# Layer 0 of a two-layer kernel: the top two experts marked in place of indexed, value products in halves

## Chip, cores and metric

The kernel runs on one core of one Trainium2 chip. The metric is device time in microseconds of one launch. The engines are TensorE (PE; its weight loads are PEld), VectorE (DVE), ScalarE (ACT), GpSimd (POOL) and SyncE (SP), which issues most transfers.

## The reference, cut

Two post-norm layers over x of 16 x 512 tokens with 128 features. The change touches layer 0 alone: an attention over the 16 heads of each token (not over tokens), and a mixture of 8 experts of which the two with the largest logits count.

```python
# attention of layer 0, per token: 16 heads of 8
q, k, v = (qkv[..., :dh], qkv[..., dh:2 * dh], qkv[..., 2 * dh:])
scores = jnp.einsum('bnhd,bngd->bnhg', q, k) / SCALE
attn = jax.nn.softmax(scores, axis=-1)
out = jnp.einsum('bnhg,bngd->bnhd', attn, v)
# experts of layer 0
logits = jnp.einsum('bsd,ed->bse', x, gate_w) + gate_b
topv, topi = jax.lax.top_k(logits, K)                       # K = 2 of E = 8
keep = jax.nn.one_hot(topi, E, dtype=jnp.float32).sum(axis=-2)
logits = jnp.where(keep > 0, logits, -jnp.inf)
gate_score = jax.nn.softmax(logits, axis=-1)
out = jnp.einsum('bseo,bse->bso', expert_out, gate_score)
```

## The kernel before

`layer0` takes the 8192 tokens as 32 pairs of tiles of 128 tokens. Each engine has its own program, written out by hand as a function `step(u, j, part)`, and 32 steps (plus the filling and the emptying) run through `steps`; the middle ones are a hardware loop of two steps a turn. The stages are skewed: in the step in which pair s gets its scores, pair s-1 gets its value products and head sums, pair s-2 its gate and experts, pair s-3 its second norm. Within one engine the order is that of the calls in its `step`; between engines semaphores decide. A name ending in `_ready`, `_ps` or `_sb` is such a semaphore.

One step on DVE (L627 and below): the moments of the first norm (L640, L644, which wait for PE's `r1_ps`), sums of the exps and their reciprocal (L736, L743, for POOL), two products of queries and keys (L662, 4.4 us together), the moments of the second norm (L652, L656), the gate (L677 to L705), the sums of the products (L714), their maximum (L720) and the shift (L727).

The gate turns the 8 logits of each token of the two tiles (`ps_logits`, a part of the PSUM tile `ps_front`) into 8 gates. It finds the 8 largest of each tile in order (`dve.max`, L677), then their indices (`max_index`, L680, which is a load of the values and a search), casts the indices to f32 (L683), compares them with an iota (L689), makes the two softmax weights out of ACT's exp of the difference of the two largest (`gexp`, L533; L685, L694, L696), multiplies (L698) and adds over the two ranks (L705). The cast indices, the denominator and the weights are kept in PSUM. PE and ACT wait for `gates_ready`: ACT scales the expert products with the gates (`apply_gates`, L542), PE makes the second tile's expert products (`four_experts`, L396) when the first four gated tiles have left PSUM.

POOL makes the attention weights (`normalise`, L266) and then, per tile, one product of weights and values of 128 x 2048 (`pv_products`, L274), and between them the small steps of the norms (L288 to L310) and the residual's bias (L316). PE adds each tile's product over the heads with 16 transposing matmuls (`sum_heads`, L364), the first of which waits for the whole product; the sum goes through ACT (`copy_oT`, L505) to the projection (`project`, L377, L379), whose result DVE's next moments read.

## Time and profile before

| | us |
|---|---|
| median of 3 runs | 2190.77 (2188.96 to 2191.76) |
| profiled execution | 2186.65 |
| its span, first to last instruction | 2184.9 |
| layer 0 in the span | about 0 to 540 |
| PE, DVE, ACT, POOL busy over the whole span | 93%, 81%, 72%, 49% |

Each engine's busy share says how full it is, not whether it sets the end. For that one reads the timeline of each engine in one step and looks for the engine that never waits for another. A record's start and duration are in us; a number in square brackets is the idle time just before it and whose work ended it. Records of one engine may overlap by some hundredths of a us, since its instructions are pipelined. A merged row (x2) covers several instructions in sequence.

### The profile page before, as it was taken

Reading aid. Unit: us, or ns where it says so; the run is one execution under the profiler, and the core shown is the slowest. Engines: PE = TensorE matmul, PEld = TensorE weight load, DVE = VectorE, ACT = ScalarE, POOL = GpSimd, SP = SyncE. Lnnn points to the kernel's source line nnn. Section 1 sums busy time; section 2 is a strip of 40 time slices with the busy share of each in tenths; the row PEclk is TensorE's granted clock in tenths of the full one; section 3 lists DMA queues with packets and bytes.
Section 4 is the critical chain, followed back from the end, with each engine's and each line's share of the span. In section 5 each row is a group of like instructions: output and inputs, shape, how many; then the busy total and the mean of one; then the engine's idle time right before and its main releaser. Section 6 shows DMA issues by size and latency. Waiting matters only on the chain. (4 is left out here: it accounts for less than half of the span.)

```text
span 2184.9 us, 59761 instructions
## 1 busy us (share of the span) xinstructions
PE 2037.5 (93%) x16112; PEld 1524.8 (70%) x16112; DVE 1778.6 (81%) x5918; ACT 1563.4 (72%) x3951; POOL 1060.6 (49%) x2184
## 2 busy tenths in 40 slices
PE   7999999997999999999999999999999993999990
PEld 5666666664776776676676677677677663999990
DVE  7999999992888888888888888888888884777765
ACT  3666566665888877887887887887878782777774
POOL 6777878783124344334334334434434435444445
PEclk9999999998999999999999999999999996999995
DMA  2000000000000000000000000000200001222227
GB/s 77 23 29 22 29 22 29 24 24 23 2 2 12 2 12 12 4 9 11 7 7 12 9 4 12 12 2 11 89 2 12 12 3 42 64 65 64 67 59 231
DMA packets 63632, 62.84 MB, mean 29 GB/s; under 512 B 9834, under 2 KB 58613, under 8 KB 62855
## 3 DMA queue, kind: packets, MB, share of 16 engines
q1 hardware_dynamic: 54906, 42.64, 6.5%
q0 software_dynamic: 8448, 16.93, 2.2%
q8 instruction: 121, 1.98, 0.4%
q14 instruction: 157, 1.29, 0.2%
HBM read 33.17 MB, written 22.69 MB: 26 GB/s over the span
## 5 line engine op out<-in xcount | busy, mean ns | idle before, releaser
L1368 DVE SCALAR_TENSOR_TENSOR restT<-ps_t,leadT 128x512 f16<-128x512 f32 (+1 forms) x768 | 458.9, 597 | 136.5 <-ACT leadT L1295 106.4
L1295 ACT ACTIVATE leadT<-ps_t 128x512 f16<-128x512 f32 (+1 forms) x768 | 402.2, 524 | 134.4 <-PE ps_t L1169 133.4
L1152 PE MATMUL ps_s<-xT_all,qm 128*128 128x512 f32 (+1 forms) x1024 | 489.9, 560 | 0.8 <-ACT qm L1276 0.8
L1169 PEld LDWEIGHTS ps_t<-ident,p 128*128 128x128 f32 x2560 | 315.4, 141 | 234.0 <-issue 169.4
L1169 PE MATMUL ps_t<-ident,p 128*128 128x128 f32 x2560 | 413.5, 276 | 8.1 <-DVE restT L1368 6.1
L1286 ACT ACTIVATE p<-ps_s,neg_max 128x512 f32<-128x512 f32 (+1 forms) x512 | 325.6, 636 | 80.8 <-DVE neg_max L1358 67.7
L988 POOL CAST v_parts<-v_all 128x36 bf16<-128x36 f32 x256 | 57.3, 224 | 610.2 <-PE ps_o L1183 609.9
L1358 DVE CUSTOM_DVE_ANT_0 ps_s<-ps_s,mask 128x512 f32<-128x512 f32 (+1 forms) x512 | 319.8, 625 | 39.4 <-PE ps_s L1152 38.2
L1152 PEld LDWEIGHTS ps_low<-xT_all,qm 128*128 128x128 f32 x1024 | 194.8, 190 | 135.7 <-issue 122.4
L1143 PE MATMUL ps_qm<-xT_all,m_all 128*128 128x512 f32 x512 | 264.0, 597 | 2.7 <-PEq L766 2.7
L274 POOL TENSOR_TENSOR pv_prod<-probs,kv 128x2048 f32<-128x2048 f32 x64 | 259.5, 4076 | 3.8 <-POOL probs L266 2.3
L1669 POOL DMA_INDIRECT results<-row_out,row_in x136 | 133.6, 983 | 159.3 <-DVE row_out L1800 150.0
L1152 PE MATMUL ps_low<-xT_all,qm 128*128 128x256 f32 (+1 forms) x1024 | 209.0, 327 | 0.0
L1276 ACT ACTIVATE qm<-ps_qm,mb_all 128x512 f32<-128x512 f32 x256 | 176.0, 687 | 44.8 <-PE ps_qm L1143 41.4
L1286 ACT ACTIVATE p<-ps_low,neg_max 128x256 f32<-128x256 f32 (+1 forms) x512 | 187.9, 427 | 0.1
L1358 DVE CUSTOM_DVE_ANT_0 ps_low<-ps_low,mask 128x256 f32<-128x256 f32 (+1 forms) x512 | 177.2, 386 | 12.6 <-PE ps_low L1152 1.8
L1790 DVE SCALAR_TENSOR_TENSOR e_hid<-e_ps_u,e_wide,e_silu 114x128 f32<-114x128 f32 x408 | 118.3, 345 | 57.8 <-ACT e_silu L1749 57.2
L542 ACT ACTIVATE gated<-ps_y,gates 128x128 f32<-128x128 f32 x512 | 141.4, 372 | 31.0 <-DVE gates L705 29.3
L1183 PE MATMUL ps_o<-v_parts,leadT 128*128 128x27 bf16 x2560 | 161.5, 175 | 0.9 <-DVE restT L1368 0.5
L1183 PE MATMUL ps_o<-v_parts,restT 128*128 128x27 bf16 x2560 | 160.6, 174 | 0.0
L1074 POOL DMA_INDIRECT rows_dram<-rows,slot_idx x128 | 128.8, 1007 | 63.8 <-issue 50.3
L1749 ACT ACTIVATE e_silu<-e_ps_g,e_wide 114x128 f32<-114x128 f32 x408 | 120.0, 365 | 52.0 <-PE e_ps_g L1702 52.0
(231 smaller groups left out, 4144.2 us busy)
## 6 DMA issues: line engine op xcount, KB each, us to landing
row_in<-rows_dram SPq DMA_DIRECT2D x136, 65.0 KB
y<-results SPq DMA_DIRECT2D x16, 512.0 KB, 5.2
xT<-in_xT SPq DMA_DIRECT2D x32, 128.0 KB, 2.1
xres<-in_xT SPq DMA_DIRECT2D x32, 128.0 KB, 2.1
xT_all<-x2T SPq DMA_DIRECT2D x32, 128.0 KB, 2.0
out_x<-x SPq DMA_DIRECT2D x16, 256.0 KB, 3.4
xT_all<-in_wide SPq DMA_DIRECT2D x1, 2760.0 KB
results<-row_out,row_in POOLq DMA_INDIRECT x136
```

What stands on the lines that cost most here:

```text
L274: pool.tensor_tensor(tile(pv_prod, a, HH * DH).rearrange("p (g h d) -> p g h d", g=H, d=DH), tile(probs, a, HH).rearrange("p (h g) -> p g ...
L542: last = act.activation(tile(gated[a], e), tile(ps_y[half], e % 4), ACT.Copy, scale=gates[:, a * E + e:a * E + e + 1])
L1143: pe.matmul(ps_qm[:, :], blk(m_all, h), xT_all[:, bass.ds(b * S, S)], start=True, stop=True).then_inc(qm_ps, 1)
L1152: mm = pe.matmul(ps_s[n], qm[j][:, n * P:(n + 1) * P], xT_all[:, bass.ds(b * S, (n + 1) * P)], start=True, stop=True)
L1169: mm = pe.transpose(ps_t[g][:, at + n * P:at + (n + 1) * P], probs[i][:, n * P:(n + 1) * P], ident[:, :])
L1183: mm = pe.matmul(out_ps[:, i, :], part[:, at + n * P:at + (n + 1) * P], v_parts[j][:, n * PARTS * PV:(n + 1) * PARTS * PV], start=(n == 0 ...
L1276: act.activation(qm[j][:, :], ps_qm[:, :], ACT.Identity, bias=mb_all[:, h:h + 1], scale=SCALE).then_inc(qm_sb, 1)
L1286: act.activation(probs[i][:, :], ps_s[i], ACT.Exp, bias=neg_max[:, i:i + 1], scale=-1.0).then_inc(probs_ready[i], 1)
L1295: act.activation(leadT[j][g][:, :], ps_t[g][:, 0:width[g]], ACT.Copy, scale=RAISE)\
L1358: dve.tensor_tensor_reduce(out=ps_s[i], in0=ps_s[i], in1=mask[:, S - n:S], scale=-1.0, scalar=3e38, op0=ALU.add, op1=ALU.min, accum_out=ne ...
L1368: dve.scalar_tensor_tensor(out=restT[j][g][:, :], in0=ps_t[g][:, 0:width[g]], scalar=RAISE, in1=leadT[j][g][:, :], op0=ALU.mult, op1=ALU.s ...
L1669: pool.indirect_dma_start(out=results[:, :], out_offset=bass.IndirectOffsetOnAxis(ap=row_in[r][:, P + 1:ROW].bitcast(U32), axis=0), in_=ro ...
```

## The change

The gate no longer looks for indices. DVE copies the logits to SBUF for ACT and the two largest of each tile into `two_tops`, whose other six places hold the constant MARK (3.4e38). `match_replace` (a load of values and a replacing pass) writes a copy of the logits in which the two largest are MARK. ACT makes, besides the two exps it made before, the negated maximum and exp(logit - maximum) for all 8 logits of each tile. DVE then compares the marked logits with MARK and multiplies with those exps in one instruction (`weighted`), and the last instruction multiplies with the reciprocal of the denominator. Denominator, reciprocal, marked logits and weighted exps are in SBUF; nothing of the gate is kept in PSUM any more but the logits.

POOL's two products per step become four of 128 x 1024, each with its own count on `pv_multiplied`; PE's sum over the heads starts when the first half of a tile is there and waits for the second ahead of its ninth matmul. All other counts of `pv_multiplied` are doubled. `iota` is replaced by a fill of `two_tops`.

```diff
+MARK = 3.4e38

...
-    HH = H * H
+    HH, HALF_G = H * H, H // 2

...
-        iota = sb("iota", [P, 2 * E * 2])

...
         x1T = sb("x1T", [P, 2 * P])
-        top, top_idx = sb("top", [P, 16]), sb("top_idx", [P, 16], U32)
-        gexp = sb("gexp", [P, 2])
-        picked, weighted = sb("picked", [P, 2 * E * 2]), sb("weighted", [P, 2 * E * 2])
+        top, two_tops, neg_top = sb("top", [P, 16]), sb("two_tops", [P, 16]), sb("neg_top", [P, 2])
+        gexp, logit_exp, logits_sb = sb("gexp", [P, 2]), sb("logit_exp", [P, 2 * E]), sb("logits_sb", [P, 2 * E])
+        marked, weighted = sb("marked", [P, 2 * E]), sb("weighted", [P, 2 * E])
+        gate_den, gate_rec = sb("gate_den", [P, 2]), sb("gate_rec", [P, 2])
...
         ps_r1, ps_logits = ps_front[:, 0:2 * P], ps_front[:, 3 * P:3 * P + 2 * E]
-        ps_idxf = ps_front[:, 3 * P + 16:3 * P + 32]
-        ps_gden, ps_gw = ps_front[:, 3 * P + 32:3 * P + 34], ps_front[:, 3 * P + 36:3 * P + 40]
...
+        neg_top_ready, logit_exp_ready = sem("neg_top_ready"), sem("logit_exp_ready")
+        logits_sb_ready, act_passed = sem("logits_sb_ready"), sem("act_passed")

...
-        GATE_STEPS = 8
+        GATE_STEPS = 6

...
                 pool.memset(eps_pair[:, :], EPS).then_inc(consts_made, 1)
-                pool.iota(iota[:, :], pattern=[[0, 2], [1, E], [0, 2]], base=0, channel_multiplier=0,
-                          allow_small_or_imprecise_dtypes=True).then_inc(consts_made, 1)
+                pool.memset(two_tops[:, :], MARK).then_inc(consts_made, 1)
...
                     pool.wait_ge(recips_ready, s + 1)
-                    when(pool, pv_multiplied, 2 * s)
+                    when(pool, pv_multiplied, 4 * s)
                     pool.tensor_tensor(by_head(probs), by_head(exps),
                                        exp_rec[:, :].unsqueeze(2).to_broadcast([P, 2 * H, H]),
                                        ALU.mult).then_inc(probs_ready, 1)
 
-                def pv_products(u, j, a):
+                def pv_products(u, j, a, half):
                     s = 2 * u + j
                     pool.wait_ge(probs_ready, s + 1)
-                    when(pool, pv_summed, 2 * (s - 1) + a + 1)
+                    if half == 0:
+                        when(pool, pv_summed, 2 * (s - 1) + a + 1)
+                        pool.sem_inc(pool_passed, 1)
                     pool.tensor_tensor(
-                        tile(pv_prod, a, HH * DH).rearrange("p (g h d) -> p g h d", g=H, d=DH),
-                        tile(probs, a, HH).rearrange("p (h g) -> p g h", h=H).unsqueeze(3)
-                        .to_broadcast([P, H, H, DH]),
-                        kv[j][:, (2 * a + 1) * P:(2 * a + 2) * P].rearrange("p (g d) -> p g d", d=DH)
-                        .unsqueeze(2).to_broadcast([P, H, H, DH]), ALU.mult).then_inc(pv_multiplied, 1)
+                        tile(pv_prod, 2 * a + half, HALF_G * P).rearrange("p (g h d) -> p g h d", g=HALF_G, d=DH),
+                        tile(probs, a, HH).rearrange("p (h g) -> p g h", h=H)[:, half * HALF_G:(half + 1) * HALF_G]
+                        .unsqueeze(3).to_broadcast([P, HALF_G, H, DH]),
+                        kv[j][:, (2 * a + 1) * P + half * HALF_G * DH:(2 * a + 1) * P + (half + 1) * HALF_G * DH]
+                        .rearrange("p (g d) -> p g d", d=DH)
+                        .unsqueeze(2).to_broadcast([P, HALF_G, H, DH]), ALU.mult).then_inc(pv_multiplied, 1)
...
                         normalise(*before(u, j, 1))
-                        pv_products(*before(u, j, 1), 0)
-                        pv_products(*before(u, j, 1), 1)
+                        for a in range(2):
+                            for half in range(2):
+                                pv_products(*before(u, j, 1), a, half)
...
                     s = 2 * u + j
-                    pe.wait_ge(pv_multiplied, 2 * s + a + 1)
+                    pe.wait_ge(pv_multiplied, 4 * s + 2 * a + 1)
                     if a == 0:
                         when(pe, oT_sb, s)
                         when(pe, x1T_sb, s)
                         when(pe, v_sb, 2 * (s - 2))
                     for g in range(H):
+                        if g == HALF_G:
+                            pe.wait_ge(pv_multiplied, 4 * s + 2 * a + 2)
...
                     s = 2 * u + j
-                    when(act, pv_multiplied, 2 * (s - 2) + a + 1)
+                    when(act, pv_multiplied, 4 * (s - 2) + 2 * a + 2)
...
                                        bias=top[:, 8 * a + 1:8 * a + 2]).then_inc(gate_exp_ready, 1)
+                    act.mul(neg_top[:, :], top[:, :].rearrange("p (a c) -> p a c", c=8)[:, :, 0], -1.0)\
+                       .then_inc(neg_top_ready, 1)
+                    act.wait_ge(logits_sb_ready, s + 1)
+                    act.sem_inc(act_passed, 1)
+                    act.wait_ge(neg_top_ready, s + 1)
+                    for a in range(2):
+                        act.activation(tile(logit_exp, a, E), tile(logits_sb, a, E), ACT.Exp,
+                                       bias=neg_top[:, a:a + 1]).then_inc(logit_exp_ready, 1)
...
                         dve.max(tile(top, a, 8), tile(ps_logits, a, E)).then_inc(tops_found, 1)
-                    wait_alone(dve, tops_found, 2 * (s + 1), passed)
-                    for a in range(2):
-                        dve.max_index(tile(top_idx, a, 8), tile(top, a, 8), tile(ps_logits, a, E))\
+                    dve.tensor_copy(logits_sb[:, :], ps_logits).then_inc(logits_sb_ready, 1)
+                    dve.wait_ge(tops_found, 2 * (s + 1))
+                    dve.tensor_copy(two_tops[:, :].rearrange("p (a c) -> p a c", c=8)[:, :, 0:2],
+                                    top[:, :].rearrange("p (a c) -> p a c", c=8)[:, :, 0:2]).then_inc(gate_step, 1)
+                    dve.wait_ge(gate_exp_ready, 2 * (s + 1))
+                    dve.tensor_scalar(gate_den[:, :], gexp[:, :], 1.0, None, ALU.add).then_inc(gate_step, 1)
+                    wait_alone(dve, gate_step, base + 1, passed)
+                    for a in range(2):
+                        dve.match_replace(tile(marked, a, E), tile(two_tops, a, 8), tile(ps_logits, a, E), MARK)\
                            .then_inc(gate_step, 1)
                     dve.wait_ge(gate_step, base + 2)
-                    dve.tensor_copy(ps_idxf, top_idx[:, :]).then_inc(gate_step, 1)
-                    dve.wait_ge(gate_exp_ready, 2 * (s + 1))
-                    dve.tensor_scalar(ps_gden, gexp[:, :], 1.0, None, ALU.add).then_inc(gate_step, 1)
-                    dve.wait_ge(gate_step, base + 3)
-                    index = ps_idxf.rearrange("p (a c) -> p a c", c=8)[:, :, 0:2]
-                    by_rank = [P, 2, E, 2]
-                    dve.tensor_tensor(picked[:, :].rearrange("p (a e r) -> p a e r", a=2, r=2),
-                                      iota[:, :].rearrange("p (a e r) -> p a e r", a=2, r=2),
-                                      index.unsqueeze(2).to_broadcast(by_rank), ALU.is_equal).then_inc(gate_step, 1)
+                    dve.reciprocal(gate_rec[:, :], gate_den[:, :]).then_inc(gate_step, 1)
+                    dve.wait_ge(logit_exp_ready, 2 * (s + 1))
+                    dve.sem_inc(passed, 1)
                     dve.wait_ge(gate_step, base + 4)
-                    weights = ps_gw.rearrange("p (a r) -> p a r", r=2)
-                    dve.reciprocal(weights[:, :, 0], ps_gden).then_inc(gate_step, 1)
+                    dve.scalar_tensor_tensor(out=weighted[:, :], in0=marked[:, :], scalar=MARK, in1=logit_exp[:, :],
+                                             op0=ALU.is_equal, op1=ALU.mult).then_inc(gate_step, 1)
                     dve.wait_ge(gate_step, base + 6)
-                    dve.tensor_tensor(weights[:, :, 1], gexp[:, :], weights[:, :, 0], ALU.mult).then_inc(gate_step, 1)
-                    dve.wait_ge(gate_step, base + 7)
-                    dve.tensor_tensor(weighted[:, :].rearrange("p (a e r) -> p a e r", a=2, r=2),
-                                      picked[:, :].rearrange("p (a e r) -> p a e r", a=2, r=2),
-                                      weights.unsqueeze(2).to_broadcast(by_rank), ALU.mult).then_inc(gate_step, 1)
-                    dve.wait_ge(gate_step, base + 8)
                     when(dve, gT_ps, s)
                     when(dve, gated_ready, 4 * s)
                     dve.sem_inc(passed, 1)
-                    dve.tensor_reduce(gates[:, :].rearrange("p (a e) -> p a e", a=2),
-                                      weighted[:, :].rearrange("p (a e r) -> p a e r", a=2, r=2), AX_X, ALU.add)\
+                    dve.tensor_tensor(gates[:, :].rearrange("p (a e) -> p a e", a=2),
+                                      weighted[:, :].rearrange("p (a e) -> p a e", a=2),
+                                      gate_rec[:, :].unsqueeze(2).to_broadcast([P, 2, E]), ALU.mult)\
```

## Rows read from the trace of the kernel before

**Rows 1.** Windows view, layer 0's loop. Columns: stretch, engines' busy time, granted clock, DMA
```profile
core 0: us, PE busy (x) PEld busy (x) DVE busy (x) ACT busy (x) POOL busy (x), PEclk, DMA share, GB/s
40.10:488.00 447.90, 420.60 (x2560) 303.06 (x2559) 417.70 (x870) 275.69 (x952) 350.61 (x345) 1.00 0.08 25
```

**Rows 2.** Timeline of DVE. Columns: start us, us, engine, line, operation, out<-in, shapes
```profile
334.61 4.43 DVE L714 TENSOR_REDUCE ps_scores<-qk_prod 128x512 f32<-128x4096 f32 x1
...
347.58 0.25 DVE L677 MAX8 top<-ps_front 128x8 f32<-128x8 f32 x2
...
348.47 0.15 DVE L685 TENSOR_SCALAR ps_front<-gexp 128x2 f32<-128x2 f32 x1
...
349.11 0.19 DVE L698 TENSOR_TENSOR weighted<-picked,ps_front 128x32 f32<-128x32 f32 x1
...
349.83 4.43 DVE L714 TENSOR_REDUCE ps_scores<-qk_prod 128x512 f32<-128x4096 f32 x1
...
355.94 0.49 DVE L640 BATCH_NORM_STATS2 stats<-ps_front 128x6 f32<-128x128 f32 x2 [0.17 <-issue]
...
365.40 4.43 DVE L714 TENSOR_REDUCE ps_scores<-qk_prod 128x512 f32<-128x4096 f32 x1
```

**Rows 3.** Timeline of PE in the same step
```profile
351.11 1.12 PE L396 MATMUL ps_y<-expw_sb,x1T 128*128 128x512 f32 x2
352.19 1.97 PE L364 MATMUL ps_turn<-ident,pv_prod 128*128 128x128 f32 x16
...
355.30 0.38 PE L379 MATMUL ps_front<-ident,xres 128*128 128x128 f32 x2
```

**Rows 4.** Timeline of ACT in the same step
```profile
347.79 0.48 ACT L533 ACTIVATE gexp<-top 128x1 f32<-128x1 f32 x2 [2.10 <-DVE top L677]
...
349.92 2.17 ACT L542 ACTIVATE gated<-ps_y,gates 128x128 f32<-128x128 f32 x8 [0.72 <-DVE gates L705]
```

**Rows 5.** Timeline of POOL, then its groups by shape: count, busy us, mean ns
```profile
344.03 8.11 POOL L274 TENSOR_TENSOR pv_prod<-probs,kv 128x2048 f32<-128x2048 f32 x2
...
L274 POOL TENSOR_TENSOR pv_prod<-probs,kv 128x2048 f32<-128x2048 f32 x64 | 259.5, 4076 | 3.8 <-POOL probs L266 2.3
...
L266 POOL TENSOR_TENSOR probs<-exps,exp_rec 128x512 f32<-128x512 f32 x32 | 34.0, 1061 | 8.2 <-DVE exp_rec L743 8.0 <-issue 0.2
...
L316 POOL TENSOR_TENSOR xres<-xres,bproj_sb 128x256 f32<-128x256 f32 x32 | 19.6, 614 | 0.0
```

**Rows 6.** Timelines of DVE and POOL in layer 1, and POOL's L988: duration min/median/max
```profile
683.97 0.22 DVE L1511 TENSOR_TENSOR masked<-place,r_picked 128x64 f32<-128x64 f32 x1
...
683.99 0.28 POOL L988 CAST v_parts<-v_all 128x36 bf16<-128x36 f32 x1 [2.95 <-PE ps_o L1183]
...
1080.60 0.27 DVE L1511 TENSOR_TENSOR masked<-place,r_picked 128x64 f32<-128x64 f32 x1
...
1080.57 0.22 POOL L988 CAST v_parts<-v_all 128x36 bf16<-128x36 f32 x1 [3.24 <-PE ps_o L1183]
...
L988 POOL CAST v_parts<-v_all x242: 219/220/291, 600.7 to 1794.6; 128x36 bf16<-128x36 f32 x121
```

**Rows 7.** Last stage: DVE and POOL side by side, and DVE's group, mean 690 ns
```profile
2150.77 0.69 DVE L1912 TENSOR_TENSOR r<-y 128x512 f32<-128x512 f32 x1
...
2150.53 1.01 POOL L1891 TENSOR_TENSOR f_rstd<-f_var,f_minus_half 128x4 f32<-128x4 f32 x1
...
L1912 DVE TENSOR_TENSOR r<-y 128x512 f32<-128x512 f32 x16 | 11.0, 690 | 17.9 <-DMA y<-results 10.3 <-ACT x L1903 7.5
```

**Rows 8.** PE's pauses in square brackets, and windows with the granted clock
```profile
518.35 2.15 PE L396 MATMUL ps_y<-expw_sb,x1T 128*128 128x512 f32 x4 [1.68 <-ACT gated L542]
...
528.92 0.69 PE L444 MATMUL ps_tail<-ident,x 128*128 128x128 f32 x2 [3.37 <-ACT x L563]
...
33.30:40.10 6.80, 5.23 (x12) 3.15 (x13) 6.39 (x16) 1.66 (x5) 6.70 (x4) 0.50 0.00 0
...
504.00:528.00 24.00, 17.44 (x102) 11.59 (x100) 4.04 (x25) 12.69 (x45) 6.53 (x17) 1.00 0.04 12
528.00:541.90 13.90, 9.07 (x15) 4.16 (x16) 1.38 (x4) 3.01 (x8) 4.71 (x26) 0.51 0.18 49
```

## The prediction

> **What bounds the kernel now.** I read the busy shares of layer 0 first: from 40 to 488 us both PE and VectorE (DVE) are busy some 94% of the time, GpSimd (POOL) 78%, ACT 62%, at a granted clock of 1.00 [rows 1]. So the layer is a loop in which several engines are nearly full, and the second view must be the order of time in one step. There DVE runs without a real hole: the big reduction L714 starts at 334.61 and, two steps later, at 365.40, so a step is 15.39 us [rows 2]. Between the first instruction of the gate (L677, 347.58) and L714 (349.83) lie 2.25 us, most of them instructions of 0.15 to 0.2 us and waits of DVE for its own last result [rows 2]. PE is almost as late: its second pair of expert products starts at 351.11, soon after ACT has made four gated tiles from 349.92 on, the head sums of the second tile at 352.19, the residual's last matmul ends at 355.68, and DVE reads that result at 355.94 [rows 2 to 4]. POOL's two value products run from 344.03 to 352.14, and the second head sum starts 0.05 us behind them [rows 3, 5]. So three paths end within 0.2 us of each other, but DVE is the one with no slack: whatever is added between L677 and L714 lengthens the step one for one, and what is taken off POOL or PE alone gives next to nothing. Layer 1 is not touched.
>
> **The profiled execution** took 2186.65 us for a span of 2184.9; the median of the runs is 4.1 us higher. I work out a difference and add it to the median, 2190.8.
>
> **Value products in halves.** POOL now issues four products of 1024 elements. Its rows are 614 ns for 256, 1061 for 512 and 4076 for 2048 elements [rows 5]; the line through the last two gives 2.06 us for 1024, that through the first and last 2.10. Four of them are 8.2 to 8.4 us for 8.15, so POOL pays 0.1 to 0.25 us a step; it is idle in 22% of the time [rows 1], so this is hidden unless POOL is the bound. In return the second head sum has only eight matmuls left behind the last product, half of the 1.97 us that its sixteen take [rows 3]. Taken alone that can free only PE's and POOL's 0.05 to 0.2 us of co-lateness, 0 to 0.1 us a step, since DVE's own chain is as long.
>
> **The gate: instruction count.** Out go the cast, the comparison, a multiply, the weighting and the reduce and the index search; in come two copies, two match-and-replace pairs (as many pairs as the search had), one two-operation instruction and a last multiply. That is one instruction less on DVE, 0.1 to 0.2 us. ACT gets three more before the gates can be made: after the two exps that start at 347.79 and last 0.48 together [rows 4] one negation (0.3), a wait for it, and two exps over 8 logits (0.48, as the two before), so the last ends about 349.05. DVE's weighting stood at 349.11 [rows 2] and would come at 349.0 now, so ACT's longer chain takes back the saved instruction: a wait of DVE of 0 to 0.3 us. Together -0.15 to +0.3 us a step, taken as 0. The iota replaced by a fill runs once. ACT's copy of the next keys and values moves back by some 0.3 us, and nobody waits for it until the next step.
>
> **The gate: where its operands lie.** This is the term that decides. Before, every small DVE instruction of the gate had at most one operand pair in SBUF (the others were in `ps_front`). After, `two_tops<-top` and `gate_den<-gexp` go from SBUF to SBUF, and `weighted<-marked,logit_exp` and `gates<-weighted,gate_rec` read two SBUF tensors, all while POOL is streaming its products. Layer 1 of this trace has such meetings in small. POOL's cast L988 takes 219 to 220 ns in nearly all of 242 cases [rows 6]. Where DVE's L1511 (two SBUF inputs, 64 elements) starts 10 to 15 ns ahead of it, it takes 0.28 us: 0.06 us more, about DVE's 64 elements. Where the cast starts 0.03 us ahead, the cast keeps its 0.22 and L1511 takes 0.27 instead of 0.22 [rows 6]. So the later one waits for the streaming of the earlier. DVE's L1912, with two SBUF inputs too, takes its usual 0.69 us beside a POOL power of 1.01 us over 4 elements [rows 7]: it is streaming that blocks, not the length of the record. A half product is 1024 elements of streaming, 2.1 us.
>
> The Trainium skill ("SBUF — State Buffer", section "Who interferes with whom") states the same as a rule: a DVE instruction with two SBUF inputs, or an SBUF-to-SBUF copy or tensor_scalar in a two-port mode, and a GpSimd instruction that reads SBUF take a shared port pair in turn, and the later one blocks for the whole of the earlier. The power in rows 7 does not bear out "whole", the small meetings bear out the rest; for products that stream throughout both readings give the same sum.
>
> **The sum for one step**, counted from POOL's first product (344.03 is 0): the products end at 2.1, 4.2, 6.3 and 8.3. The gate starts at 3.55 and L714 stood at 5.80 [rows 2]. The copy of the two tops is ready at 3.9 and waits until 4.2. The denominator (before at 348.47, so 0.9 us behind L677) comes at 4.4, into the third product: until 6.3, then 0.15. Matches 0.4 and the reciprocal 0.15 to 0.2: 7.0. The weighting then meets the fourth product and waits until 8.3 to 8.4; from its start to L714 0.72 us, as from L698 to L714 before [rows 2]: 9.1. That is +3.3 us. Bounds: only one product waited for, L714 at 7.7, +1.9 us; POOL keeps the port between its products, so that the first waiter stays until 8.3 and all the rest, 2 us, follows: +4.5 us. Products of 31 of the 32 steps lie beside a gate (the last gate has none): 31 x 3.3 = 102 us.
>
> **PE's pause.** PE then waits over 3.3 us in each step for the first gated tiles, in place of none ahead of 351.11 [rows 3]. In the trace a pause of 3.37 us (ends 528.92) lies where the clock has fallen to 0.51, while the stretch before, with 73% busy but only pauses up to 1.7 us, kept 1.00; in 33.3 to 40.1 it was 0.50, too [rows 8]. At 1.2 in place of 2.4 GHz PE's work takes double, and the 4.6 us of it from the second experts (351.11) to the residual's end (355.68) would come out behind DVE. Lower bound nothing; upper bound a low stretch as long as that one in each step, 3.4 us, 105 us in all. The nearest row is the pause behind which the clock fell, as long as the new one, but such a stretch falls anywhere in a step, and part of it meets slack: I take 1.0 us a step, 31 us. Sum: 102 + 31 = 133; 2190.8 + 133 = 2324 us.
>
> **The rivals.** (a) No block: POOL's long product gives way between pieces of its stream, and the meetings cost 0.05 us as the small ones. Then only the terms above are left, -0.15 to +0.3 us a step, 2186 to 2200 us, most likely 2190. For it: no row shows a meeting with a long product. Against: rows 6, in both directions. This is the side on which it is not slower; it turns faster if DVE's saved instruction and the earlier head sum both count, -0.2 us a step, 2185. (b) One block only, since small copies take the narrow way or the second meeting falls between products: +1.9 us a step and little of the clock, 2245 to 2275. (c) POOL keeps its port to the end of the fourth product: 4.5 us a step and the clock, 2330 to 2400. (d) The block as summed, but PE keeps 2.4 GHz: 2293. (e) The block as summed and a low clock in nearly every step, over 2 us each: 2355 to 2395.
>
> **How the numbers follow.** The block as summed with part of the clock's price, 0.42, with (d) 0.17 beside it and (e) 0.09; (b) 0.11; (c) 0.08; (a) 0.13. The range 2240 to 2370 takes in the forecast, (d), (b), half of (c) and of (e), and leaves out (a): some 0.2 is outside. What a measurement of this kernel can tell from no change is about 0.2%, 4.4 us. Only (a) gives faster (0.03) or the same (0.10, with the tail of its slow end in slower): slower 0.87.
>
> **What would show it.** If right: mean durations of the denominator and of the weighting near 2 us or a hole of that size before them, L677 to L714 over 5 us, `gates` ending with POOL's fourth product, PE idle over 3 us before the second expert products, and granted clock below 1.00 somewhere between 60 and 500 us. POOL's halves at 2.05 to 2.15 us with only small delays. Wrong if those two DVE instructions stand at 0.15 to 0.2 us beside running products: then the step stays near 15.4 us. Wrong in size only if the clock row reads 1.00 throughout, or if one of the two instructions is short.

## The result and the profile after

The changed kernel took 2303.56 us, median of 4 runs (2300.73 to 2304.64), beside 2189.86 us (2188.49 to 2191.76) for the kernel before on the same chip: 1.052 times as long, 95% interval 1.0506 to 1.0535, so 113.7 us more. Forecast were 133 us more. The profiled execution has a span of 2301.3 us against 2184.9.

All of it arises in layer 0. Layer 1's first masked maximum on DVE starts at 539.05 us before and at 655.47 after, and from there to the end of the span it is 1645.9 and 1645.8 us. Of the 116.4 us by which the profiled span is longer, 97.6 lie between the fifth L714 (L723) and the last, which are 27 steps, 12.7 ahead of them and 6.2 in the emptying of the pipeline behind them.

Two questions are open to the profile: how much longer is a step, and what does DVE do in it. The windows view comes first, as in rows 1: the whole loop of layer 0, then two neighbouring steps, then the stretch in the first of these two in which the clock is low.

```profile
core 0: us, PE busy (x) PEld busy (x) DVE busy (x) ACT busy (x) POOL busy (x), PEclk, DMA share, GB/s
44.20:598.00 553.80, 444.85 (x2562) 330.14 (x2560) 505.77 (x842) 289.33 (x1039) 360.12 (x405) 0.95 0.06 20
369.20:388.84 19.64, 15.99 (x88) 12.08 (x88) 17.33 (x30) 10.04 (x36) 12.38 (x15) 0.91 0.06 20
388.84:406.99 18.15, 14.33 (x88) 10.53 (x88) 17.38 (x30) 9.93 (x36) 12.39 (x15) 1.00 0.07 22
371.90:375.30 3.40, 3.40 (x16) 3.22 (x15) 3.16 (x4) 2.03 (x8) 0.00 (x0) 0.50 0.00 0
```

DVE is nearly as full as before (91% beside 93%), but by instructions that wait inside their own records; PE fell from 94% to 80%. The granted clock, 1.00 in rows 1, is 0.95: stretches at 0.50 (1.2 GHz, half of the 2.4 that 1.00 stands for) come back all through the loop. The next view is DVE's timeline through one gate, the counterpart of rows 2 (start, duration, engine, line, operation; waits in brackets).

```profile
349.37 4.41 DVE L723 TENSOR_REDUCE ps_scores<-qk_prod 128x512 f32<-128x4096 f32 x1
...
364.24 0.25 DVE L691 MAX8 top<-ps_front 128x8 f32<-128x8 f32 x2
...
364.53 0.58 DVE L694 COPY two_tops<-top 128x4 f32<-128x4 f32 x1
365.02 0.15 DVE L697 TENSOR_SCALAR gate_den<-gexp 128x2 f32<-128x2 f32 x1
...
365.77 1.44 DVE L707 SCALAR_TENSOR_TENSOR weighted<-marked,logit_exp 128x16 f32<-128x16 f32 x1
367.45 1.82 DVE L713 TENSOR_TENSOR gates<-weighted,gate_rec 128x16 f32<-128x16 f32 x1 [0.24 <-DVE weighted L707]
369.20 4.41 DVE L723 TENSOR_REDUCE ps_scores<-qk_prod 128x512 f32<-128x4096 f32 x1
...
388.84 4.41 DVE L723 TENSOR_REDUCE ps_scores<-qk_prod 128x512 f32<-128x4096 f32 x1
```

And POOL's and ACT's beside it, the counterparts of rows 5 and 4:

```profile
360.86 8.38 POOL L276 TENSOR_TENSOR pv_prod<-probs,kv 128x1024 f32<-128x1024 f32 x4 [0.28 <-POOL probs L266]
...
365.06 0.49 ACT L547 ACTIVATE logit_exp<-logits_sb,neg_top 128x8 f32<-128x8 f32 x2
```

Read them together. POOL's four halves start at 360.86 and take 8.38 us, so one ends about every 2.09 us: by their single records at 363.00, 365.09, 367.17 and 369.24. The copy of the tops starts before the second of these moments and its record ends at 365.11. The weighting starts at 365.77 and ends at 367.21, just behind the third. The last multiply starts at 367.45 and ends at 369.27, just behind the fourth. An instruction of 16 elements takes 1.44 or 1.82 us, and its end is set by POOL's instruction, not by its own work. The denominator is short: it went through at 365.02, at the same boundary between two products at which the copy came free. `logit_exp` ends at 365.55, ahead of the weighting, so ACT's longer chain isn't what DVE waits for. From L691 to L723 it is 4.96 us where rows 2 had 2.25: 2.71 more. That it is so in nearly every step is read from DVE's and POOL's groups (busy us, mean ns):

```profile
L713 DVE TENSOR_TENSOR gates<-weighted,gate_rec 128x16 f32<-128x16 f32 x32 | 53.8, 1680 | 7.4 <-DVE weighted L707 7.3
L707 DVE SCALAR_TENSOR_TENSOR weighted<-marked,logit_exp 128x16 f32<-128x16 f32 x32 | 45.7, 1429 | 1.8 <-ACT logit_exp L547 0.2
L694 DVE COPY two_tops<-top 128x4 f32<-128x4 f32 x32 | 20.0, 625 | 0.2 <-issue 0.2
L697 DVE TENSOR_SCALAR gate_den<-gexp 128x2 f32<-128x2 f32 x32 | 9.0, 281 | 0.3 <-ACT gexp L539 0.3
...
L276 POOL TENSOR_TENSOR pv_prod<-probs,kv 128x1024 f32<-128x1024 f32 x128 | 268.1, 2126 | 7.4 <-POOL probs L266 7.4
```

The denominator's mean of 281 ns hides two gates out of 32 (its median is 155). There it took 2.18 and 2.16 us. The first of the two:

```profile
460.30 2.18 DVE L697 TENSOR_SCALAR gate_den<-gexp 128x2 f32<-128x2 f32 x1
...
462.78 1.77 DVE L707 SCALAR_TENSOR_TENSOR weighted<-marked,logit_exp 128x16 f32<-128x16 f32 x1
464.79 0.21 DVE L713 TENSOR_TENSOR gates<-weighted,gate_rec 128x16 f32<-128x16 f32 x1 [0.25 <-DVE weighted L707]
```

Here the denominator meets the third product and the weighting the fourth, as the prediction's sum had it, the last multiply is nearly free, and the gate is 5.60 us. Its start lies within 0.03 us of the third product's, as in the steps in which it passed: which of the two patterns a step gets is decided by hundredths of a us.

What the late gate does to PE, the counterpart of rows 3, in two neighbouring steps:

```profile
350.82 1.55 PE L402 MATMUL ps_y<-expw_sb,x1T 128*128 128x512 f32 x2 [2.89 <-ACT gated L556]
352.17 3.20 PE L370 MATMUL ps_turn<-ident,pv_prod 128*128 128x128 f32 x16
...
370.66 1.13 PE L402 MATMUL ps_y<-expw_sb,x1T 128*128 128x512 f32 x2 [3.22 <-ACT gated L556]
371.62 3.37 PE L370 MATMUL ps_turn<-ident,pv_prod 128*128 128x128 f32 x16
...
376.91 0.49 DVE L654 BATCH_NORM_STATS2 stats<-ps_front 128x6 f32<-128x128 f32 x2 [1.78 <-PE ps_front L385]
```

PE waits 2.89 and 3.22 us for the gated tiles, and behind that wait its sixteen head sums take 3.20 and 3.37 us instead of 1.97 [rows 3]. DVE gets the residual late: it waits 1.78 us where rows 2 show 0.17. So there are two kinds of steps: about 18.0 to 18.15 us from L723 to L723 where the clock stays up, and 19.6 to 19.8 (349.37, 369.20, 388.84) where a low stretch falls on the work that DVE needs next. Of the last 27 steps 12 are of the first kind (the very last has 18.27) and 15 of the second (one of them 20.29, the one with the long gate). Each of these 15 holds one low stretch, the 12 others none. The pause before it does not tell which it will be: 2.89 us ahead of 350.82 in a long step, 3.03 ahead of 390.30 in a short one.

### The profile page after: what moved, and what is told of

Read it like the earlier page. It is cut to its first block and busy times, and to the rows that moved or that the text cites. A ratio compares the mean times of both kernels' runs of the same rounds, so it can differ in the third digit from the quotient of the medians.

```text
span 2301.3 us, 59994 instructions
## 1 busy us (share of the span) xinstructions
PE 2069.7 (90%) x16112; PEld 1559.2 (68%) x16112; DVE 1872.2 (81%) x5886; ACT 1578.2 (69%) x4047; POOL 1066.2 (46%) x2248
## 5 line engine op out<-in xcount | busy, mean ns | idle before, releaser
L276 POOL TENSOR_TENSOR pv_prod<-probs,kv 128x1024 f32<-128x1024 f32 x128 | 268.1, 2126 | 7.4 <-POOL probs L266 7.4
L402 PE MATMUL ps_y<-expw_sb,x1T 128*128 128x512 f32 x256 | 140.3, 652 | 96.2 <-ACT gated L556 96.2
L370 PEld LDWEIGHTS ps_turn<-ident,pv_prod 128*128 128x128 f32 x1024 | 142.7, 163 | 30.9 <-issue 27.0
```

The costliest lines, as they stand in the source:

```text
L276: pool.tensor_tensor(tile(pv_prod, 2 * a + half, HALF_G * P).rearrange("p (g h d) -> p g h d", g=HALF_G, d=DH), tile(probs, a, HH).rearran ...
L370: mm = pe.matmul(tile(ps_oT, a), tile(pv_prod, a * H + g), ident[:, :], start=(g == 0), stop=(g == H - 1), is_transpose=True)
```

## Experiments

Theory A: DVE's instructions with two SBUF inputs, or from SBUF to SBUF, stand until POOL's running product is done, and PE's pause then costs clock. Rival B: the new gate is longer by its own chain (matches, ACT's exps), wherever its operands lie. Rival C: PE's clock is a by-product that costs nothing. Of the halves it was said that POOL hides them. Ratios are against runs of the kernel before that were taken together with each experiment's: their median was 2188.8 to 2190.4 us, and 2194.6 for the old gate in SBUF and the three versions with the copy put later. So the ratios compare, and the times of these four stand some 4 us too high beside the others.

**Marks and weighting in PSUM.** The changed kernel, but for where two buffers lie.

```diff
-        marked, weighted = sb("marked", [P, 2 * E]), sb("weighted", [P, 2 * E])
+        marked, weighted = ps_front[:, 3 * P + 16:3 * P + 32], ps_front[:, 3 * P + 32:3 * P + 48]
```

> The changed kernel with marked and weighted in PSUM (in ps_front, where the old gate had its small tiles), so that neither the weighting nor the last gate instruction has two SBUF inputs; everything else, the wait for ACT's exps too, stays. Theory (DVE waits for the product that POOL is streaming): both instructions fall from 1.4 and 1.8 us to 0.2, L691 to the scores' reduction from 4.96 to 2.2 to 2.6 us (the copy of the tops still meets a product, 0.4 us), a step of 15.4 to 15.7 us, 2188 to 2202 us in all, clock 1.00 in the loop. Rival (the new wait for ACT's exps, or the two operations in one instruction, are slow by themselves): nothing moves, 2295 to 2305 us.

Measured: 2204.91 us, 1.0068 (1.0051 to 1.0086). DVE's timeline of this kernel, the same two instructions:

```profile
361.84 0.18 DVE L707 SCALAR_TENSOR_TENSOR ps_front<-ps_front,logit_exp 128x16 f32<-128x16 f32 x1
...
362.27 0.17 DVE L713 TENSOR_TENSOR gates<-ps_front,gate_rec 128x16 f32<-128x16 f32 x1 [0.25 <-DVE ps_front L707]
```

They take 0.18 and 0.17 us beside running products where they took 1.44 and 1.82, with the same operations, elements and order. The gate is 2.25 us again and 98.7 of the 113.7 us are gone. That decides between A and B. (PE's pause goes with the blocks, so the 98.7 hold the clock's price as well.) But the time is slightly above what was expected, and a step is 15.8 us though the gate is as short as before; something else costs 0.4 us.

**Only the marks in PSUM.** `weighted` stays in SBUF, so that the weighting no longer reads two SBUF tensors and the last multiply still does.

```diff
-        marked, weighted = sb("marked", [P, 2 * E]), sb("weighted", [P, 2 * E])
+        weighted = sb("weighted", [P, 2 * E])
+        marked = ps_front[:, 3 * P + 16:3 * P + 32]
```

> The changed kernel with only marked in PSUM: the weighting has one SBUF input, the last gate instruction keeps two. Theory of the streaming: the weighting falls to 0.2 us, the last instruction comes about 5.3 us behind POOL's first product, in the third, and waits about 1 us for its end at 6.3, so the gate takes 3.1 to 3.3 us, a step 16.2 to 16.4 us, 2212 to 2225 us in all. If instead a contended instruction costs a fixed 1.5 to 1.8 us each: gate 3.5 us, 2230 us or more. If the weighting's wait only moves to the last instruction, until the fourth product ends: 2295 to 2305 us.

Measured: 2208.7 us, 1.0099 (1.0064 to 1.0133), a little less than expected. DVE and POOL of this kernel:

```profile
360.51 0.18 DVE L708 SCALAR_TENSOR_TENSOR weighted<-ps_front,logit_exp 128x16 f32<-128x16 f32 x1
360.93 1.03 DVE L714 TENSOR_TENSOR gates<-weighted,gate_rec 128x16 f32<-128x16 f32 x1 [0.25 <-DVE weighted L708]
...
355.62 8.39 POOL L277 TENSOR_TENSOR pv_prod<-probs,kv 128x1024 f32<-128x1024 f32 x4 [0.20 <-POOL probs L267]
```

The third product ends at 355.62 + 3 x 2.1 = 361.9; the multiply starts at 360.93 and ends at 361.96. It meets the product that the weighting met, and waits for its end instead. The gate is 2.90 us, 0.65 more than before. The run is 19.9 us longer than the kernel before, which looks like 31 x 0.65 and isn't: with both in PSUM, and a gate of 2.25, it was 16.1 longer already. Beside that version a step grows by only 0.2 us (15.8 to 16.0), because DVE waited 0.62 and 0.56 us for the projection there, in two neighbouring steps, and 0.18 us or nothing here. And in two gates of this profile the denominator missed its gap and took 2.19 us; they are 4.97 us long. An instruction's block is the rest of the product in which it falls, so blocks can't be added up as fixed prices: take one away and the next instruction meets another part of the stream.

**The gate alone, products whole.** The kernel before with the new gate, without the halves.

```diff
-                        for a in range(2):
-                            for half in range(2):
-                                pv_products(*before(u, j, 1), a, half)
+                        pv_products(*before(u, j, 1), 0)
+                        pv_products(*before(u, j, 1), 1)
```

> The changed gate with POOL's whole products and the head sums as before. Theory of the streaming: the weighting meets the second whole product and waits for its end, 8.15 us behind the start of the first, over 3 us; the last instruction then meets none. The gate takes 5.2 to 5.5 us, 0.2 to 0.5 more than with halves, and PE pauses longer: 2300 to 2325 us. Rival (the four half products are themselves what costs, by their number or by what they do to DVE): nearer to the kernel before, under 2290 us.

Measured: 2328.67 us, 1.064 (1.0622 to 1.0657), longer than the full change by 25 us and slightly above what was expected, and it isn't the weighting that waits. DVE and POOL:

```profile
359.50 0.26 DVE L688 COPY two_tops<-top 128x4 f32<-128x4 f32 x1
359.94 3.84 DVE L691 TENSOR_SCALAR gate_den<-gexp 128x2 f32<-128x2 f32 x1 [0.18 <-ACT gexp L533]
...
364.09 0.17 DVE L701 SCALAR_TENSOR_TENSOR weighted<-marked,logit_exp 128x16 f32<-128x16 f32 x1
...
355.66 8.10 POOL L274 TENSOR_TENSOR pv_prod<-probs,kv 128x2048 f32<-128x2048 f32 x2
```

The first product ends at 359.7, between the copy's start and the denominator's. The denominator then takes 3.84 us for two elements, until 363.78, where POOL's second product ends (355.66 + 8.10 = 363.76). Behind it nothing streams, and the weighting takes 0.17. Here the tensor_scalar, short in the changed kernel, carries the whole block: which instruction waits depends on where each falls, and how long on what is left of POOL's instruction. The gate is 5.61 us where 5.2 to 5.5 were expected.

**The old gate with its operands in SBUF.** No new operation at all: the kernel before, with three of its small buffers moved out of `ps_front`.

```diff
-        ps_idxf = ps_front[:, 3 * P + 16:3 * P + 32]
-        ps_gden, ps_gw = ps_front[:, 3 * P + 32:3 * P + 34], ps_front[:, 3 * P + 36:3 * P + 40]
+        ps_idxf, ps_gden, ps_gw = sb("idxf", [P, 16]), sb("gden", [P, 2]), sb("gw", [P, 4])
```

> The kernel before, its old gate instruction for instruction, with whole products; only the cast indices, the denominator and the two weights lie in SBUF in place of PSUM. Theory (it is the place of the operands, not the new gate): the cast comes some 4.3 us behind the start of POOL's first product, into the second, and waits for its end at 8.1; the rest of the gate follows, so the gate takes 5.7 to 6.1 us in place of 2.25, PE pauses over 3.5 us and the clock falls in part of the steps: a step of 19 to 21 us, 2320 to 2370 us. Rival (the marked gate is slow for another reason): 2188 to 2200 us.

Measured: 2350.22 us, 1.0708 (1.0692 to 1.0724), as expected: more than the change itself costs. DVE and POOL:

```profile
344.56 3.75 DVE L682 CAST idxf<-top_idx 128x16 f32<-128x16 uint32 x1
348.36 0.18 DVE L688 TENSOR_TENSOR picked<-iota,idxf 128x32 f32<-128x32 f32 x1
...
340.16 8.12 POOL L273 TENSOR_TENSOR pv_prod<-probs,kv 128x2048 f32<-128x2048 f32 x2 [0.18 <-POOL probs L265]
```

The cast of 16 numbers ends at 348.31, POOL's last product at 348.28. The same cast in the kernel before, written to PSUM beside a running product:

```profile
348.39 0.18 DVE L683 CAST ps_front<-top_idx 128x16 f32<-128x16 uint32 x1
```

Place is enough; marks or indices don't matter.

**No meeting at all, in halves and whole.** All operands of the new gate are laid so that no DVE instruction of it reads two SBUF tensors or copies from SBUF to SBUF; ACT then reads `two_tops`, and waits for the copy into it (in lines left out here).

```diff
-        top, two_tops, neg_top = sb("top", [P, 16]), sb("two_tops", [P, 16]), sb("neg_top", [P, 2])
+        two_tops, neg_top = sb("two_tops", [P, 16]), sb("neg_top", [P, 2])
...
-        gate_den, gate_rec = sb("gate_den", [P, 2]), sb("gate_rec", [P, 2])
+        gate_rec = sb("gate_rec", [P, 2])
...
+        marked, weighted = ps_front[:, 3 * P + 16:3 * P + 32], ps_front[:, 3 * P + 32:3 * P + 48]
+        top, gate_den = ps_front[:, 3 * P + 48:3 * P + 64], ps_front[:, 3 * P + 64:3 * P + 66]
```

> The changed kernel with every small operand of the gate placed so that no DVE instruction has two SBUF inputs or copies from SBUF to SBUF: the tops are found into PSUM, copied once to SBUF (ACT reads them there), marks, weighted and denominator in PSUM. Streaming theory with POOL's end on the path: the copy of the tops falls from 0.58 to 0.2 us, the gate takes 1.8 to 2.1 us, but the step stays at 15.7 to 15.9 us, since POOL's halves bound it: 2198 to 2206 us. If DVE alone bounded it (the prediction's reading): step 15.0 to 15.2, 2178 to 2186 us.

> The same gate without meetings, with POOL's whole products and the head sums as before. If POOL's halves are what costs the rest: a step of 15.15 to 15.4 us, 2178 to 2190 us, the gate 1.8 to 2.1 us. If the marked gate itself (ACT's three more instructions, the order of its copies) costs: 2195 us or more.

Measured: with halves 2200.42 us, 1.005 (1.0035 to 1.0064); with whole products 2191.12 us, 1.0003 (0.9994 to 1.0012). DVE of the latter:

```profile
354.01 0.16 DVE L692 TENSOR_SCALAR ps_front<-gexp 128x2 f32<-128x2 f32 x1 [0.55 <-ACT gexp L534]
...
355.24 0.17 DVE L708 TENSOR_TENSOR gates<-ps_front,gate_rec 128x16 f32<-128x16 f32 x1 [0.25 <-DVE ps_front L702]
```

Every instruction is short, but ACT's exp now comes behind the copy, and DVE waits 0.55 us for it: the gate is 2.52 us, not the 1.8 to 2.1 that I had expected, and the time isn't below before's. In this layout, choosing the experts by marks costs nothing that can be measured and brings nothing; what is left in the version with halves, 0.5%, belongs to the halves. The version with whole products also shows how much slack DVE has in the kernel before: there the gate takes 2.25 and 2.37 us in turn, so 2.52 is some 0.2 more, and a step is 15.44 us beside 15.39. Most of the 0.2 us is absorbed.

**The halves alone.** The kernel before, with only the products and the head sums' waits changed.

```diff
-                        pv_products(*before(u, j, 1), 0)
-                        pv_products(*before(u, j, 1), 1)
+                        for a in range(2):
+                            for half in range(2):
+                                pv_products(*before(u, j, 1), a, half)
```

> The kernel before with POOL's products in halves and the head sums begun at the first half, the old gate untouched. The prediction's reading: the 0.1 to 0.25 us a step that POOL pays is hidden, the earlier head sums free 0 to 0.1 us: 2186 to 2192 us. New theory, from the kernel with the marks in PSUM (there ACT's copy of the second tile's keys and values waited 0.6 us for POOL's last product, and DVE 0.6 us for the projection): ACT's order puts that copy ahead of the head sums' copy, so the end of the fourth product is on the path of every step whatever the head sums do, and POOL's 0.28 us a step with what it shifts is added whole: a step of 15.7 to 15.85 us, 2196 to 2206 us.

Measured: 2200.95 us, 1.0053 (1.0039 to 1.0067). POOL, ACT, PE and DVE of this kernel, in the order in which one releases the other:

```profile
339.18 8.40 POOL L276 TENSOR_TENSOR pv_prod<-probs,kv 128x1024 f32<-128x1024 f32 x4 [0.28 <-POOL probs L266]
...
347.69 0.37 ACT L505 COPY kv<-ps_qkv 128x256 f32<-128x256 f32 x1 [0.50 <-POOL pv_prod L276]
...
350.31 0.68 PE L383 MATMUL ps_front<-wproj_sb,attnT 128*128 128x128 f32 x4 [0.37 <-ACT attnT L511]
...
351.40 0.50 DVE L646 BATCH_NORM_STATS2 stats<-ps_front 128x6 f32<-128x128 f32 x2 [0.54 <-PE ps_front L385]
```

The gate is 2.25 us as before, yet the steps are 15.68 and 15.98, 0.44 more on average. POOL's products take 8.40 instead of 8.11, and their end is on the path after all: ACT's copy of the next keys and values waits for POOL (the buffer is still being read), ACT's `attnT` copy stands behind it, then PE's projection, then DVE's moments, which wait 0.54 us where rows 2 have 0.17.

**That copy put later.** If ACT's waiting copy is the link, moving it behind the `attnT` copy must give the halves back.

```diff
-                    if part[0]:
-                        copy_kv(*before(u, j, -1), 1)
...
+                    if part[0]:
+                        copy_kv(*before(u, j, -1), 1)
```

> The kernel before with halves, and ACT's copy of the second tile's keys and values put behind its copy of the head sums. Theory (that copy, which must wait for POOL's last product, stood in front of the head sums' copy and turned POOL's extra 0.28 us into the step's length): the step falls from 15.83 to 15.3 to 15.5 us, 2184 to 2194 us, as the kernel before or a little faster. Rival (POOL's end binds in another way, as by its own next work): still 15.7 us or more, 2198 us or more.

> The marked gate without meetings, halves, and ACT's copy of the keys and values later. Theory: DVE alone bounds the step, with a gate of 2.5 us (it waits 0.55 us for ACT's first exps), 15.35 to 15.5 us: 2186 to 2195 us, where the same kernel with ACT's old order took 2200. Rival: ACT's order is not it, 2198 us or more.

> The kernel before with ACT's copy put later and nothing else, the control for the two others. DVE bounds the step and the copy waits at most 0.16 us in every second step: 0 to 0.1 us a step less, 2185 to 2191 us. If POOL's last product bounds the kernel before as well: 2180 us or less.

Measured: the halves alone with the copy later 2202.96 us, 1.0039 (1.0025 to 1.0053); the gate without meetings, in halves, 2205.26 us, 1.0044 (1.0031 to 1.0057); the control, before with only this move, 2195.73 us, 0.9999 (0.999 to 1.0007). The first two miss what I expected of them: a step is 15.73 and 15.71 us, where the move was to bring it to 15.3 to 15.5. The control's 2195.73 lies above the 2185 to 2191 expected only because its set stands higher. POOL, ACT and DVE of the first:

```profile
343.59 0.20 POOL L313 TENSOR_TENSOR shift<-mean,rstd 128x2 f32<-128x2 f32 x1
...
343.90 0.81 ACT L569 ACTIVATE x<-ps_tail,shift,rstd 128x128 f32<-128x128 f32 x2 [0.42 <-POOL shift L313]
344.60 0.37 ACT L511 COPY attnT<-ps_turn 128x256 f32<-128x256 f32 x1
...
346.30 0.49 DVE L646 BATCH_NORM_STATS2 stats<-ps_front 128x6 f32<-128x128 f32 x2 [0.47 <-PE ps_front L385]
```

The move gave back only 0.1 us a step, because a second link lay behind the first, by this trace nearly as long: POOL makes the norm's `shift` right behind its products, ACT's norm (L569) waits 0.42 us for it, in front of the same `attnT` copy, and DVE still waits 0.47 us. So the trace has POOL's end bind by two waits of ACT, of which only one was freed; that freeing both would do it is argued from here and not shown.

**PE kept busy in its pause.** The changed kernel with idle matmuls (their result is overwritten; nothing of the computation is left out) ahead of the expert products that wait for the gates: first 24, then 12.

```diff
+                    if part[2] and part[3]:
+                        for n in range(12):
+                            pe.matmul(ps_turn[:, 3 * P:4 * P], ident[:, :], ident[:, :], start=True, stop=True)
```

> The changed kernel with 24 idle transposing-size matmuls (about 2.6 us at 2.4 GHz) into unused columns of ps_turn, put where PE pauses some 3 us for the first gated tiles. Theory (the pause brings TensorE's clock down, and the steps of 19.6 to 19.8 us beside those of 18.0 to 18.2 are that): granted clock 1.00 in the loop, all steps 18.0 to 18.2 us, 2303 less some 15 x 1.65 and some more at the start, 2265 to 2282 us. Rival (the clock falls for another reason, or the long steps have another cause): two lengths of step stay, 2295 us or more.

> The changed kernel with 12 idle matmuls in PE's pause in place of 24; the 24 took 5.4 us, two passes of 0.11 us each, and overran the pause of 3.1 us by 1.9 us, though the granted clock was 1.00 in the loop. 12 take 2.7 us and fit. Theory (the pause brings the clock down and the long steps are that): clock 1.00 in the loop, all steps 18.0 to 18.3 us, 2265 to 2285 us. Rival: two lengths of step stay, 2295 us or more.

Measured: with 24, 2331.45 us, 1.0649 (1.0632 to 1.0667), against expectation; with 12, 2273.35 us, 1.0377 (1.0359 to 1.0396), as expected. The windows and PE's timeline of the first, then of the second:

```profile
46.00:630.00 584.00, 566.60 (x3975) 464.86 (x3974) 504.59 (x842) 289.89 (x1039) 358.93 (x403) 1.00 0.06 19
...
388.54 5.52 PE L483 MATMUL ps_turn<-ident 128*128 128x128 f32 x48
...
398.40 0.50 DVE L657 BATCH_NORM_STATS2 stats<-ps_front 128x6 f32<-128x128 f32 x2 [2.02 <-PE ps_front L385]
```

```profile
44.90:573.00 528.10, 497.33 (x3283) 389.94 (x3281) 505.91 (x843) 288.06 (x1039) 360.95 (x404) 1.00 0.07 21
...
354.57 2.84 PE L483 MATMUL ps_turn<-ident 128*128 128x128 f32 x24
...
357.78 1.12 PE L402 MATMUL ps_y<-expw_sb,x1T 128*128 128x512 f32 x2 [0.36 <-ACT gated L559]
358.74 1.91 PE L370 MATMUL ps_turn<-ident,pv_prod 128*128 128x128 f32 x16
```

In both the granted clock rounds to 1.00 over the loop. Each of the 24 matmuls is recorded as two passes of some 0.11 us: 48 of them, 5.52 us for a pause of about 3, so that PE came late by its own filling and DVE waited 2.02 us. Twelve take 2.84 us and fit: the wait left is 0.36 us, the sixteen head sums take 1.91 us again, and the last 27 steps are 17.9 to 18.2 us. The gates' meetings are as in the changed kernel, so the difference, 2303.6 - 2273.4 = 30 us, is what the clock's falls cost: 25.0 us of it in these 27 steps, most of the rest in the emptying. Rival C is out.

None of the twelve beats the kernel before; the nearest are the gate without meetings and with whole products (1.0003) and the control (0.9999), neither of which can be told from it.

## Why the prediction was right, and where its steps failed

The direction, the range and the mechanism held: 113.7 us more, 133 forecast. The pattern of the waits within a gate did not, and the clock's term came out right in part by luck. Term by term:

- **Where the operands lie: right.** Moving `marked` and `weighted` gives back 98.7 us; moving three buffers of the old gate the other way costs 7.1%. Rival (a), no block, is out. The Trainium skill ("SBUF — State Buffer", section "Who interferes with whom") says that the later of the two instructions waits for the whole of the earlier. For POOL's streaming products the trace agrees: 3.84, 3.75, 1.82 and 1.44 us, each ending within 0.05 us of a product's end.
- **Which instruction waits: the failed step.** The prediction let the denominator "come at 4.4, into the third product". It came at 365.02, 4.16 us behind POOL's start, when the copy was being let through (product's end at 4.23, the copy's at 4.25), and took 0.15. The 0.9 us that I had put behind the gate's start came from L685, which in the old gate stands behind the searches and the cast; ACT's exps are done 0.7 us behind it already in rows 4, and that is where the new gate's order puts the denominator. With the denominator gone through, the weighting met the third product and the last multiply the fourth, which I had thought free behind the weighting. So two instructions waited as forecast, but others, and the last block ended with POOL's last product rather than one chain of 0.72 us behind it: L723 at 8.34 instead of 9.1. In the two gates in which the denominator did miss the gap, the pattern is the forecast one and so is its price: 5.60 us in the one shown, 3.35 more than before, for 3.3.
- **The size.** The gate grew by 2.71 us, not 3.3; 31 x 2.71 = 84 us instead of 102. The run at full clock has just that: 2273.4 - 2190.4 = 83 us, of which the last 27 steps, at 2.69 each, hold 72.6. These 18 us are nearly the whole difference between forecast and result. The end by rival (c), POOL keeping the port over all its products, is out: there are gaps between its instructions, and DVE passes in them.
- **The denominator as a risk: right in kind.** With whole products it waited 3.84 us. That it mostly didn't in the changed kernel is a matter of at most 0.2 us: it starts 0.16 to 0.25 us behind the second product's start in the gate alone, where it waited 3.83 to 3.93, and within 0.03 us of the third's in the changed kernel.
- **PE's pause and the clock: right in kind, the number in part by luck.** A pause of over 3.3 us was forecast; it is 2.89 and 3.22 us in the two steps shown. The clock's price was put at 31 us, 1.0 us in each of 31 steps, a choice between 0 and 105 that no row gave, and came out at 30. It is made up otherwise: 15 of the last 27 steps are longer by some 1.65 us each and 12 not at all, and the emptying adds 4.6 us. Rival (d), the clock staying up, is what the run with 12 idle matmuls made.
- **The instruction count: right.** Taken as 0; the gate without meetings and with whole products stands at 1.0003. ACT's longer chain ends 1.31 us behind L691 (1.47 forecast) and DVE isn't held by it.
- **The halves, "hidden": wrong.** POOL's extra was sized well (8.38 for four, forecast 8.2 to 8.4), but its place was misread. I argued from POOL's idle 22% and from DVE's full chain that 0.1 to 0.25 us of it cost nothing. Alone it costs 0.44 us a step in the profile, 10.6 us by the medians. The share of idle time is an average: POOL is idle elsewhere, while its products' end is waited for by ACT in two places. Nor was DVE the one engine without slack: in rows 2 it stands idle for 0.17 us ahead of its moments, a gap that the profile puts down to no engine, and in the gate without meetings and with whole products 0.2 us more of gate cost only 0.05 us a step. So "whatever is added between L677 and L714 lengthens the step one for one" holds for the large block, not for the first tenths of a us, and PE's path, which hangs on POOL's end, is as late as DVE's. In the changed kernel this is masked, because the gate's 2.71 us make DVE's chain the longest: at full clock the step is longer by 2.7 us and no more. The halves even help there, by cutting the block: 2328.7 with whole products, 2303.6 with halves.

What stays open: POOL's 0.29 us more make 0.44 us of a step in the version with halves alone, and the 0.15 beyond it were not found. Nor was a version tried in which both of ACT's waits are moved.

## What to carry to other kernels

While GpSimd streams from SBUF, an instruction of VectorE that reads two SBUF tensors, or copies, casts or adds a constant (tensor_scalar) from SBUF to SBUF, costs the rest of GpSimd's instruction, here with 2 elements as with 16; put one operand or the result of small chained steps into PSUM, and look at where a change puts its buffers before counting its instructions. What a block costs depends on where in the other engine's instruction it falls, so lay the two timelines over each other, instruction by instruction, and move every later instruction along with it. And "hidden" needs a row that shows who waits for the end of the work, not a share of idle time.

## What the runs showed of the hardware

- DVE's turn comes at the boundary between two GpSimd instructions, though they follow each other without a pause: the copy ended at 365.11 and the denominator at 365.17, with a product's end at 365.09. One boundary let through two instructions, 0.15 us the second, in 29 of the 31 gates beside products; in the two others the second waited 2.18 and 2.16 us.
- Not every instruction from SBUF to SBUF waits: the reciprocal of the denominator (`gate_rec`, L703) starts at 365.55, inside the third product, and takes 0.15 us, as in all 32 gates (148 to 157 ns). The add on the same two elements took 3.84 us in the gate alone.
- The wait is inside the record: the profile calls DVE busy for 1.44, 1.82 or 3.84 us and names no releaser. A mean duration far above that of a sister instruction of the same shape (1680 ns beside 0.17 us in PSUM) is the only mark it leaves.
- The work behind the pause pays for a clock fall. PE's sixteen head sums take 3.20 and 3.37 us where a stretch at 1.2 GHz falls on them and 1.91 at 2.4, and a pause filled with 2.84 us of idle matmuls kept the clock at 1.00 and won 30 us. Filling past the pause's end lost all of it again: 2331 us.
